# A gate that reads its PSUM bank: moving one copy off ScalarE in a Mamba-2 mixer stage

## The reference, cut to what matters

```python
proj = einsum('bld,pd->blp', hidden, W_in)       # gate 2048, hBC 2304, dt 32
hBC  = silu(causal_conv4(hBC) + conv_b)          # xs (32 heads x 64), B, C (128 each)
dt   = softplus(dt + dt_bias);  dA = exp(dt * -exp(A_log))
h    = dA * h + (dt * x) B^T;   y = h C          # over 256 positions, per head
y    = y + D * xs
g    = y * silu(gate)
g    = g * rsqrt(mean(g * g) + eps) * norm_w
out  = einsum('bli,di->bld', g, W_out)
```

## Time and profile before

| | |
|---|---|
| time, median of 3 runs | 1452.89 us (1442.77 to 1454.18) |
| profiled execution, span from first to last instruction | 1444.4 us; no other time of that execution is given, and this lies inside the runs' range |
| mean granted clock of TensorE | 0.952 |
| busy of the span: PE, DVE, ACT, POOL | 84%, 61%, 41%, 39% |
| the copy of `pg` on ACT (line 737) | 32 executions, 587 to 592 ns |

### The profile page before, as it was taken

The page is one execution under the profiler, slowest core; times in us unless marked ns, Lnnn a source line. Parts: engine busy times, 40 slices in busy tenths (PEclk is TensorE's granted clock), DMA queues, the critical chain, the costliest instruction groups (busy, mean ns, idle before and its releaser), DMA issues. The chain is left out here.

```text
span 1444.4 us, 16409 instructions
## 1 busy us (share of the span) xinstructions
PE 1208.4 (84%) x4614; PEld 641.6 (44%) x4614; DVE 879.5 (61%) x1244; ACT 593.9 (41%) x1742; POOL 569.6 (39%) x531
## 2 busy tenths in 40 slices
PE   0048899779897699999986898988799787997998
PEld 0014444334453344444434555643485336844443
DVE  7978999389985564246325948729741496504222
ACT  2025454454454232232224546647672476711110
POOL 5562675626665231002002856727651275500000
PEclk9999999999999799999998999989899898997999
DMA  6000000000003400000003000030000000000000
GB/s 253 0 22 1 0 1 1 1 0 0 0 0 120 157 0 1 0 0 0 33 10 136 1 1 0 0 138 1 1 2 1 1 0 0 0 0 8 0 0 29
DMA packets 5481, 33.24 MB, mean 23 GB/s; under 512 B 528, under 2 KB 1936, under 8 KB 3536
## 3 DMA queue, kind: packets, MB, share of 16 engines
q1 hardware_dynamic: 5424, 32.61, 5.8%
HBM read 31.56 MB, written 1.05 MB: 23 GB/s over the span
## 5 line engine op out<-in xcount | busy, mean ns | idle before, releaser
L813 POOL TENSOR_TENSOR decays<-decays,scores 128x768 f32<-128x768 f32 x64 | 124.8, 1953 | 152.0 <-ACT decays L749 152.0
L575 PE MATMUL pg<-h,weights 128*128 (+1 forms) x136 | 66.5, 612 | 85.5 <-PEq L356 82.6
L1998 POOL TENSOR_TENSOR f_pair<-m,weights 128x256 f32<-128x256 f32 x80 | 90.9, 1156 | 92.6 <-DVE m L2019 91.6
L1101 PE MATMUL ph<-h,weights 128*128 x256 | 116.5, 600 | 0.0
L1406 POOL TENSOR_TENSOR prob_latent<-prob_latent,inverse_latent 128x128 f32<-128x128 f32 (+1 forms) x128 | 81.5, 660 | 70.4 <-DVE inverse_latent L1396 70.1
L575 PE MATMUL px<-h,weights 128*128 x136 | 73.3, 664 | 26.1 <-DVE conv L886 26.0
L749 ACT ACTIVATE decays<-pcum,neg_cum 128x256 f32<-128x256 f32 (+1 forms) x256 | 87.7, 449 | 11.4 <-PE pcum L628 11.2
L1246 DVE TENSOR_TENSOR mid<-up,ph 128x512 f32<-128x512 f32 x44 | 30.2, 687 | 98.5 <-ACT up L1158 98.5
L1406 POOL TENSOR_TENSOR prob_gqa<-prob_gqa,inverse_gqa 128x128 f32<-128x128 f32 (+1 forms) x128 | 62.0, 506 | 58.4 <-DVE inverse_gqa L1396 56.8
L1158 ACT ACTIVATE up<-ph 128x512 f32<-128x512 f32 x44 | 26.3, 597 | 140.4 <-PE ph L1101 140.4
L886 DVE SCALAR_TENSOR_TENSOR conv<-px,pp,conv 128x510 f32<-128x510 f32 (+2 forms) x102 | 75.1, 737 | 14.5 <-ACT conv L714 11.6
(11 more groups left out here) (327 smaller groups left out, 3069.6 us busy)
## 6 DMA issues: line engine op xcount, KB each, us to landing
weights<-in_w_mixer SPq DMA_DIRECT2D x2, 2048.0 KB, 18.3
weights<-in_w_moe SPq DMA_DIRECT2D x2, 1536.0 KB, 7.8
moe_rest<-in_w_moe SPq DMA_DIRECT2D x2, 1536.0 KB, 13.9
weights<-in_w_gqa SPq DMA_DIRECT2D x1, 3072.0 KB, 10.2
weights<-in_w_gqa SPq DMA_DIRECT2D x1, 2048.0 KB, 14.7
weights<-in_w_moe SPq DMA_DIRECT2D x1, 1920.0 KB, 9.1
weights<-in_w_mixer SPq DMA_DIRECT2D x1, 1536.0 KB, 11.8
weights<-in_w_moe SPq DMA_DIRECT2D x1, 1152.0 KB, 11.7
```

The source lines that it names most:

```text
L575: op = nc.tensor.matmul(out[0:m, :], w[:, col + k * m:col + (k + 1) * m], net.h[:, ds(i * PAIR + k * TOK, TOK)], start=(k == 0), stop=(k = ...
L813: nc.gpsimd.tensor_tensor(decays[:, head % 4], decays[:, head % 4], scores[:], ALU.mult).then_inc(decay_scaled, 1)
L1101: op = nc.tensor.matmul(out[:], wt[:, n * D + k * P:n * D + (k + 1) * P], net.h[:, ds(i * PAIR + k * TOK, TOK)], start=(k == 0), stop=(k = ...
L1998: op = nc.gpsimd.tensor_tensor(out[:, :, s, :], src[:, :, 1 - s, :], sin[:, None, s, :].to_broadcast([P, 4, HALF]), ALU.mult)
```

## The change

`tanh_gate` no longer copies `pg`: `silu_gate` on DVE reads `pg` itself, and its end now gives the bank back to PE. `gated` writes y = D xs + `py` back into the bank `py`, and the multiplication by the gate reads it there; the bank is free for the next `mix` once `g` is made. The waits of `tanh_gate` on the slots of `gate` go; it waits for `pg_free` of the step before.

```diff
-                    project(x_bank(n), P, col, i, y_free, px_ready, i * N)
+                    project(x_bank(n), P, col, i, g_ready, px_ready, i * N)
...
-                pe.wait_ge(y_free, i * N + s)
+                pe.wait_ge(g_ready, i * N + s)
...
-                act.wait_ge(gate_ready, i * N + s)
-                if s >= 4:
-                    act.wait_ge(g_ready, i * N + s - 3)
-                elif s == 0:
-                    act.wait_ge(parts_ready, i + 1)
-                else:
-                    act.wait_ge(pt_ready, i * (N + 2) + 1)
+                act.wait_ge(pg_free, i * (N + 1) + s + 1)
                 nc.scalar.activation(tanh_g[:], pg[:], ACT.Tanh, scale=0.5) \
                     .then_inc(tanh_g_ready, 1)
-                nc.scalar.activation(gate[:, s % 4, :], pg[:], ACT.Copy).then_inc(pg_free, 1)
...
                 dve.wait_ge(tanh_g_ready, i * N + s + 1)
-                dve.wait_ge(pg_free, i * (N + 1) + s + 2)
-                v.scalar_tensor_tensor(gate[:, s % 4, :], tanh_g[:], 1.0, gate[:, s % 4, :],
-                                       ALU.add, ALU.mult).then_inc(gate_ready, 1)
+                v.scalar_tensor_tensor(gate[:, s % 4, :], tanh_g[:], 1.0, pg[:],
+                                       ALU.add, ALU.mult).then_inc(pg_free, 1)
...
-                v.scalar_tensor_tensor(y[:], xs[:, s % 4, :], net.pp[:, PP_D + s:PP_D + s + 1],
-                                       py[:], ALU.mult, ALU.add).then_inc(y_free, 1)
-                dve.wait_ge(y_free, i * N + s + 1)
+                v.scalar_tensor_tensor(py[:], xs[:, s % 4, :], net.pp[:, PP_D + s:PP_D + s + 1],
+                                       py[:], ALU.mult, ALU.add).then_inc(y_made, 1)
+                dve.wait_ge(y_made, i * N + s + 1)
...
-                dve.wait_ge(gate_ready, i * N + s + 1)
-                v.tensor_tensor(g[:, s % 2, :], y[:], gate[:, s % 4, :], ALU.mult) \
+                dve.wait_ge(pg_free, i * (N + 1) + s + 2)
+                v.tensor_tensor(g[:, s % 2, :], py[:], gate[:, s % 4, :], ALU.mult) \
                     .then_inc(g_ready, 1)
```

More of the change, by code:

```diff
@@ L534, in stage_mixer @@
         row_cols_ready = sem("row_cols_ready")
-        tanh_g_ready, gate_ready = sem("tanh_g_ready"), sem("gate_ready")
+        tanh_g_ready = sem("tanh_g_ready")
         decay_scaled = sem("decay_scaled")
-        y_ready, y_free, g_ready = sem("y_ready"), sem("y_free"), sem("g_ready")
+        y_ready, y_made, g_ready = sem("y_ready"), sem("y_made"), sem("g_ready")
         square_ready, square_used = sem("square_ready"), sem("square_used")
```

## The result

The changed kernel takes 1464.14 us (median of 15 runs, 1457.98 to 1469.64) against 1449.50 (15 runs, 1440.99 to 1460.57) for the kernel before on the same chip: a ratio of 1.0099 with an interval of 1.0077 to 1.0120. On a second occasion it was 1.0144 (1.0106 to 1.0182). So the change makes the kernel about 1% slower. The forecast was 1457 in a range of 1442 to 1476, with 0.75 on "within 1%", 0.18 on slower: the time lies in the range and the sign of the sum is right, but the loss is about three times the +4.6 that was worked out. Part of the nearness is luck: counted from the 1449.50 of these runs the sum gives 1454, 10 us short, and "within 1%" holds at 1.0099 by a hair and not at 1.0144.

A forecast was written before the change was run, and what follows sets the result against it. PE bounds some steps, DVE others. Per pair -0.9 + 1.1 + 5.0 - 2.9 = +2.3, two pairs +4.6: span 1444.4 becomes 1449.0, with the median 8.5 above the span 1457 us, range 1442 to 1476.

The forecast's parts named there:

- start of a pair: At each pair's start, gate's 0.49 wait for the copy and a PE spread's 0.38 for decays go: -0.9 us per pair.
- the loop, eleven periods: y to gate on DVE, pg to px on PE, back to y: 10.25 us per step, +1.1 per pair.
- xs held up: DVE's xs, two SBUF tiles, now in the closed loop, is delayed by POOL's ops: +5.0 us per pair, between 0 and 11 x 1.8.
- ACT's exponentials late in the first of the eleven: First period of a pair; the prediction has no term for it.
- clock inside the periods: PE clock drop inside the steps; given no size, named only as a sign that the forecast is wrong.
- end of a pair: After the last pg, decays come earlier and PE's half clock mostly goes: -2.9 us per pair, between -0.85 and -3.95.
- y in PSUM: 0: DVE's y writing the PSUM bank costs nothing: 0, with one hand-over of 0.11 per period either way, 2.4 us.
- The hold-up in every period: Slower rival, 0.20: POOL delays xs in all eleven periods, 11.5 us more per pair, 1480; average wait 0.9 decides the sign.
- No hold-up at all: Faster rival, 0.20: POOL delays nothing on DVE and the clock stays up, -3.8 us per pair, 1445.
- the hidden copy: Rival, 0.10: ACT's copy and the wait for pg are both hidden, only the pairs' starts remain, -1.8, 1451.

The follow-up runs named there:

- e2: Only y written to and read from the py bank, ScalarE's copy of pg kept, against the kernel before: ratio 0.9914.
- e5: Changed kernel with the short POOL op (GpSimd multiplies 8 of 128 columns of the decays): eleven periods 118.24 and 117.71 us, one run.
- e6: Kernel before with GpSimd multiplying only 8 of 128 columns of the decays: eleven periods 105.49 and 105.48 us, one run.
- e4: Kernel before with silu_gate moved ahead of silu_x in DVE's order, copy of pg kept: ratio 1.0003.
- e1: Only silu_gate reading and freeing pg, copy gone, y kept in SBUF, against the kernel before: ratio 1.0378.
- e7: Changed kernel with g's wait on tanh_g_ready in place of pg_free, except each pair's last tile: eleven periods 117.94 and 117.96 us, one run.
- e10: Changed kernel with g's wait on tanh_g_ready in place of pg_free, the same program as e7, timed: ratio to the kernel before 1.0051.

## Why the prediction was right in sign and range, and short in size

Per pair, forecast against measured (first and second pair):

| step of the prediction | forecast | measured |
|---|---|---|
| start of a pair | -0.9 | -1.4, -0.1 |
| the loop, eleven periods | +1.1 | +1.6 (11 x 10.29 = 113.2) |
| xs held up | +5.0 | +5.9, +5.6 |
| ACT's exponentials late in the first of the eleven | 0 | +0.8 |
| clock inside the periods | 0 | +1.7, 0 |
| end of a pair | -2.9 | -2.0, -1.7 |

**The loop** was right: its chain, its order, and 10.25 against 10.29. The 0.04 are 0.09 for the wait ahead of g less small change. "y in PSUM: 0" was right for the write (0.754 us, and 0.752 in e2, against 0.745) but missed that the change puts another wait there.

**xs takes over the hold-up** was the largest term and its size right to a fifth: 5.9 and 5.6 us in eleven periods, counted from 0.68 each. That is in good part luck, for its places were half right. In the first pair the last four of the eleven lose 0.65 to 0.76 each, where 1.0 had been put three times and 1.5 once, and the first loses nothing, where 0.5 had been put: 2.9 of the 5.0. The other 3.0 come in four steps that were not foreseen, 1.64 of it in one (the 2.32 above).

**The step that failed** is the sum of the loop and of what is held up inside it: no price for the clock, and none for exponentials that come late. The prediction named a drop "inside the steps" only as what would make it wrong, and gave it no price. In the first pair the 2.32 of xs cost 1.64 us of waiting and 1.7 of half clock. The sum 113.2 + 5.9 + 0.8 + 1.7 = 121.6 meets the 121.83 of the first pair, and 113.2 + 5.6 + 0.8 = 119.6 the 119.84 of the second. The 0.8 is the first period: 11.08 in the changed kernel, 10.30 with the short POOL op. There PE's second spread waits for ACT's exponentials, which are late because DVE's conv before y is late; and that is late because two ops of the next stage's condition ahead of it, `euk` (line 263), take 4.02 us (order of time of the changed kernel, DVE and PE, then the same op before):

```profile
122.46 4.02 DVE L263 TENSOR_SCALAR euk<-f,pp 128x514 f32 x2
...
134.44 0.39 PE L626 MATMUL pcum<-parts,sel 96*128 96x512 bf16 x1 [0.43 <-ACT decays L742]
```

```profile
124.11 0.88 DVE L263 TENSOR_SCALAR euk<-f,pp 128x514 f32 x2
```

They run beside POOL's decays; with the short POOL op they take 0.88 and the period 10.30. So this too is a hold-up by POOL, of an op that the prediction did not look at.

**The end of a pair** was a third or more too good: the half clock that was to be gone still comes, for less long, after a wait of 2.07 us for the gate op where 1.5 had been put down. **The start** was right for the first pair only.

These terms are the mixer's +13.5. Against the forecast's +4.6 they leave +8.9, in which no single term stands out: half clock 1.7, late exponentials 1.6, xs 1.5, loop 1.0, ends 2.1, start 0.3, and some 0.7 in small differences.

**The rivals.** The hold-up in every period (+11.5 more per pair) did not come: in the first pair three of the eleven xs are at 0.68 and one at 0.84, and the average wait is 0.54. (The 0.9 per period at which the prediction lets it decide the sign is where its sum passes 1%; the sign itself turns at 0.25.) It came in the gate half alone, where g is held up beside xs, and there it went past that price, to 136. No hold-up at all is refuted by the 1126 ns; the hidden copy by the 26 waits of PE and by e5 against e6.

On who holds up whom, the Trainium skill (SBUF — State Buffer, section "Who interferes with whom") says that a VectorE instruction with at most one SBUF input, outside some modes, does not contend with GpSimd, and that one with two contends with a GpSimd instruction that reads SBUF. These traces agree: gate 1187 to 673 ns when one input moved to PSUM, g 844 to 691, and xs, with two, up to 2.32 us and 0.55 beyond POOL's op. An op with one SBUF tile can be held up as well: `euk`, 0.48 us when free, takes 2.03 to 2.07; whether it runs in one of those modes no trace shows. The Trainium skill's rule of 120 against 58 cycles (VectorE: DVE Perf Modes, section on the TRN2 errata), which the prediction set aside, is not seen here: gate takes 673 ns with an operand in PSUM, no more than the 680 to 690 of undisturbed ops with two SBUF tiles.

**What stays open.** The +5.2 us behind the mixer. All eight profiles of kernels with both halves of the change have 969.0 to 970.2 us there, the four of before, e2, e4 and e6 964.7 to 966.0, e1 967.2. The instructions are the same and so are their waits; most of the difference sits in two places of later stages where PE's clock falls (a stretch of 50 us, columns as in the earlier trace rows, then a row of PE; first after and then before):

```profile
1143.31:1193.31 50.00, 41.90 (x122) 20.40 (x123) 33.80 (x49) 31.79 (x150) 24.47 (x22) 0.87 0.00 1
...
1339.98 5.29 PE L1093 MATMUL ph<-h,f 128*128 x8
```

```profile
1129.68:1179.68 50.00, 43.08 (x128) 21.06 (x129) 35.89 (x51) 33.98 (x160) 26.78 (x24) 0.91 0.00 0
...
1322.86 3.60 PE L1101 MATMUL ph<-h,f 128*128 x8
```

0.87 against 0.91 is 2 us of full speed in that stretch, and set side by side the rows of the two kernels drift apart by 2.1 us in its first half; at its start PE waits 5.74 us, before 4.89. The eight matmuls of the other place take 1.7 us longer, and the drift there is 2.4. Why the program that runs ahead decides it was not tried.

## What to carry to other kernels

An op that is taken off an idle engine is not free if it was what gave a buffer back: look for the op that gives it back afterwards, write down the loop that runs through both engines, and add up its links. Then look at what lies in the loop ahead of that op, for every delay of those ops is now in the period; here moving the op ahead of its neighbours turned 1.0% slower into 0.8% faster. That is no more than the y half gives alone: the copy taken off ACT gained nothing that these runs can tell. And test a change of two halves half by half: here one gained 0.9%, and the other lost 3.8% alone.

## What the runs showed of the hardware that was not expected

- A wait that counts 17 a pair, in place of one that counts 16, put 0.09 us between two dependent DVE ops (0.87 against 0.79, in one trace). Both semaphores had long been at their values. It stands behind the wait for y; the same wait ahead of the gate op in the kernel before, where nothing had to be finished first, left no gap in the rows (x_tok to gate 0.60). No run changes the count alone, so that it is the count and not the semaphore is not shown.
- An op of DVE with one SBUF tile and a scalar, `euk`, took 2.07 and 2.03 us beside POOL's decays in the changed kernel, and 0.48 in the kernel before and with the short POOL op.
- DVE writes and reads the same PSUM bank in one op in 0.754 us, against 0.745 for the form that writes SBUF.
- The same wait of PE (2.63 and 2.62 us for the gate op, in the fourth period) was followed by half clock in the first pair, pg 2.90 and then 3.68 us in the two executions of the changed kernel, and in neither execution in the second pair (of the first execution):

```profile
362.09 2.31 DVE L888 SCALAR_TENSOR_TENSOR xs<-tanh_x,conv 128x512 f32<-128x512 f32 x1
365.66 1.98 PE L575 MATMUL pg<-h,weights 128*128 x4 [2.62 <-DVE gate L893]
```

  (order of time of the changed kernel.) So the length of the wait alone does not decide it; what else does is open. The ends of e7 and e10, one program, say the same: behind a wait of 1.40 and 1.41 us the output projection took 3.32 us in the one and 1.88 in the other. A forecast can only put such a loss, 1.7 us here, into the range.
